# The products of probabilities and values: one block of 512 queries in the middle of a unit, or two of 256 behind every second score tile

## What is computed

```python
keys = jnp.einsum('bthk,hik->bthi', xd, tokeys) * scale
queries = jnp.einsum('bthk,hik->bthi', xd, toqueries) * scale
values = jnp.einsum('bthk,hik->bthi', xd, tovalues)
dot = jnp.einsum('bqhs,bkhs->bhqk', queries, keys)
attn = jax.nn.softmax(dot, axis=-1)
out = jnp.einsum('bhqk,bkhs->bqhs', attn, values).reshape(b, t, e)
```

## Time and profile before

| what | value |
|---|---|
| median of 3 runs | 4097.41 us |
| the runs | 4089.57 to 4101.62 us |
| the profiled execution, its time | 4100.87 us |
| its span | 4099.1 us |
| mean granted clock over the span | 0.972 |

### The profile page before, as it was taken

The page is one execution under the profiler, slowest core; times in us unless marked ns, Lnnn a source line. Parts: engine busy times, 40 slices in busy tenths (PEclk is TensorE's granted clock), DMA queues, the critical chain, the costliest instruction groups (busy, mean ns, idle before and its releaser), DMA issues. The chain is left out here.

```text
span 4099.1 us, 68353 instructions
## 1 busy us (share of the span) xinstructions
PE 3909.5 (95%) x23166; PEld 1958.1 (48%) x23166; DVE 3234.2 (79%) x3515; ACT 2628.8 (64%) x4939; POOL 455.0 (11%) x402
## 2 busy tenths in 40 slices
PE   8799899999999999999999999999998778999998
PEld 6587233333333333333333333333333656888887
DVE  6566799999898999989999989999971837765665
ACT  3454687878778787877878787788874432223333
POOL 0133100000000000000000000000001217001323
PEclk9899999999999999999999999999995888999999
DMA  4800321121021121113112112200012003004332
GB/s 146 226 21 16 107 30 19 12 24 28 9 30 27 9 25 21 21 12 34 21 9 28 26 10 23 31 9 6 9 29 54 26 0 107 1 1 133 77 84 37
DMA packets 301695, 157.53 MB, mean 38 GB/s; under 512 B 218397, under 2 KB 273507, under 8 KB 298800
## 3 DMA queue, kind: packets, MB, share of 16 engines
q1 hardware_dynamic: 289072, 142.49, 18.5%
q0 software_dynamic: 12288, 10.70, 1.6%
HBM read 86.46 MB, written 64.18 MB: 37 GB/s over the span
## 5 line engine op out<-in xcount | busy, mean ns | idle before, releaser
L1207 ACT ACTIVATE probs<-attention_scores_t_sums 128x512 f32<-128x512 f32 x4096 | 2126.2, 603 | 572.2 <-PE attention_scores_t_sums L1134 565.5
L1241 DVE TENSOR_REDUCE max_parts<-attention_scores_q_sums 128x1 f32<-128x1024 f32 x1008 | 1188.6, 1219 | 135.1 <-PE attention_scores_q_sums L1128 134.3
L1241 DVE TENSOR_REDUCE attention_max_parts<-attention_scores_q_sums 128x1 f32<-128x1024 f32 x992 | 1168.9, 1220 | 121.9 <-PE attention_scores_q_sums L1128 121.9
L1134 PE MATMUL attention_scores_t_sums<-q_operand,k_operand 50*128 50x512 f32 x2048 | 821.7, 469 | 14.9 <-ACTq L1221 14.0
L1134 PE MATMUL attention_scores_t_sums<-attention_q_operand,attention_k_operand 50*128 50x512 f32 x2048 | 827.3, 477 | 6.9 <-ACT probs L1207 6.9
L1128 PE MATMUL attention_scores_q_sums<-attention_k_operand,attention_q_operand 48*128 48x512 f32 x2048 | 666.5, 440 | 6.5 <-DVE max_parts L1241 2.6
L1128 PE MATMUL attention_scores_q_sums<-k_operand,q_operand 48*128 48x512 f32 x1952 | 636.7, 441 | 11.9 <-issue 5.7
L1128 PEld LDWEIGHTS attention_scores_q_sums<-attention_k_operand,attention_q_operand 48*128 48x128 f32 x2048 | 301.6, 185 | 576.8 <-DVE max_parts L1241 287.6
L1142 PE MATMUL attention_o_psum_sums<-probs,attention_v_heads 128*32 128x512 f32 x4104 | 564.7, 623 | 0.0
L1128 PEld LDWEIGHTS attention_scores_q_sums<-k_operand,q_operand 48*128 48x128 f32 x1952 | 289.1, 185 | 557.2 <-DVE max_parts L1241 273.4
L1142 PE MATMUL attention_o_psum_sums<-probs,v_heads 128*32 128x512 f32 x4096 | 545.5, 605 | 0.3 <-ACT o_parts L1203 0.3
(11 more groups left out here) (322 smaller groups left out, 4621.2 us busy)
## 6 DMA issues: line engine op xcount, KB each, us to landing
o_other_half<-o_parts SPq DMA_DIRECT2D x130, 64.0 KB, 2.0
expert_rows<-attention_empty_rows SPq DMA_DIRECT2D x16, 516.0 KB, 5.6
v_scratch<-value_chunk SPq DMA_DIRECT2D x16, 512.0 KB, 5.1
w_whole<-in_L_ffn_ew SPq DMA_DIRECT2D x8, 1024.0 KB, 7.2
experts_w_whole<-in_L_ffn_ew SPq DMA_DIRECT2D x8, 1024.0 KB, 5.7
q_operand<-q_scratch SPq DMA_DIRECT2D x24, 256.0 KB, 5.3
k_operand<-k_scratch SPq DMA_DIRECT2D x24, 256.0 KB, 6.5
attention_q_operand<-q_scratch SPq DMA_DIRECT2D x24, 256.0 KB, 4.8
```

The source lines that it names most:

```text
L1134: nc.tensor.matmul(ST[bank_n][:, :], KOP[b][64 * h:64 * h + ROWS + 2, kt * P:(kt + 1) * P], QOP[b][64 * h:64 * h + ROWS + 2, c * CH:(c + 1 ...
L1207: nc.scalar.activation(PR[:, tile, :], ST[bank_n][:, :], ACT.Exp).then_inc(st_free, 1)
L1241: nc.vector.tensor_reduce(MPART[par][:, h, u // 4, u % 4:u % 4 + 1], SA[h][:, :], AX.X, ALU.max)\
```

## The change

`pv_unit` becomes `pv_half`, which makes the products for 256 of the 512 queries (`side` 0 or 1). It is called behind each half of a unit, with the half's number as the side. Each call waits on ACT's count; the wait for the copy and for the values stays ahead of the first block of a round's first unit. The flag that clears the sums (`start`) is set in side 0 of unit 0 only, `pv_done` is counted behind side 1 only. The other engines' programs are the same.

```diff
-            def pv_unit(b, u, exps):
+            def pv_half(b, u, exps, side):
                 pe.wait_ge(st_free, NB + exps)
+                queries = slice(side * (CH // 2), (side + 1) * (CH // 2))
                 for t in range(4):
                     h, kt = 1 - t // 2, 2 * u + t % 2
-                    mm = nc.tensor.matmul(OP[32 * (2 * h + t % 2):32 * (2 * h + t % 2) + 32, :], VH[b][:, kt, h, :],
-                                          PR[:, u % 4 * 4 + t, :], start=(u == 0), stop=(u == U - 1))
-                mm.then_inc(pv_done, 1)
+                    mm = nc.tensor.matmul(OP[32 * (2 * h + t % 2):32 * (2 * h + t % 2) + 32, queries], VH[b][:, kt, h, :],
+                                          PR[:, u % 4 * 4 + t, queries], start=(u == 0 and side == 0),
+                                          stop=(u == U - 1 and side == 1))
+                if side == 1:
+                    mm.then_inc(pv_done, 1)
...
-                    if half == 0:
-                        if u == 1:
-                            pe.wait_ge(o_copied, g + 1)
-                            if r % NQ == 0:
-                                pe.wait_ge(v_in[r // NQ % 2], (i + 1) * 16)
-                        pv_unit((r - (u == 0)) // NQ % 2, (u - 1) % U, count(i, r, u - 2, 3) + 1)
+                    if half == 0 and u == 1:
+                        pe.wait_ge(o_copied, g + 1)
+                        if r % NQ == 0:
+                            pe.wait_ge(v_in[r // NQ % 2], (i + 1) * 16)
+                    pv_half((r - (u == 0)) // NQ % 2, (u - 1) % U, count(i, r, u - 2, 3) + 1, half)
...
-            pv_unit(1, U - 1, count(NP // 2 - 1, HALF - 1, U - 2, 3) + 1)
+            for side in range(2):
+                pv_half(1, U - 1, count(NP // 2 - 1, HALF - 1, U - 2, 3) + 1, side)
```

## The result

The changed kernel takes 3952.65 us in the median (3947.95 to 3957.45, 4 runs) against 4099.51 for the kernel before (4089.57 to 4102.72, 4 runs). The ratio is 0.9646, with a 95% interval of 0.9625 to 0.9666. The profiled execution took 3956.84 us, 144.0 less than the profiled one before.

A forecast was written before the change was run, and what follows sets the result against it. It took a loop of t2, exponential, t1 and products, 2.61 us a unit, to bound the kernel. 161 - 13 - 4.5 = 144 us less than 4100.87 gave 3957, the median 3.5 lower: 3954 us, range 3885 to 4015.

The forecast's parts named there:

- The loop before: Attention unit of the kernel before: t2, its exponential, t1, products; 1.18 + 0.42 + 1.00 = 2.60 us, the period.
- The half at full clock: Half an attention unit on PE: 0.65 us to the products plus a 0.57 us block, so a unit of 2.45.
- the term of 161 us: Gain in the attention at full clock: 2.61 - 2.45 = 0.16 us a unit, times 1006 units.
- The readers: DVE and ACT reading PE's banks: 0.4 and 0.15 us to spare, so PE itself becomes the bound.
- the sign that the prediction named: In the changed unit's timeline: DVE's idle spread over both reductions, about 0.08 us each.
- unchanged sums of ACT and DVE in the page: In the profile page: ACT's and DVE's busy sums stay the same over a shorter span.
- ACT's idle time in two parts a unit: In the changed unit's timeline: ACT idle about 0.2 us twice.
- the negated maxima's rows come in time: Row loads made half a round ahead stay hidden as eight units shrink from 20.9 to 19.6 us; cost nothing.
- The round's end: Accumulator copy and pushed exponentials delay two blocks, 0.25 us together, 0.21 more than now; times 63 rounds, 13 us.
- The last units: Last 18 attention units, without max scores, at half clock: 4.32 us a unit against 4.07, 4.5 us more.
- its second rival: Clock holds in the last units since PE stalls less: 34 us less, 3920 us; chance 0.12.
- The half at 1.2 GHz: Half a unit in the last units at half clock: 2.15 to 2.16 us, a unit 4.32.

The follow-up runs named there:

- short_exp: Kernel before, with ACT's exponentials over 256 of the 512 queries and the other probabilities constant: 3932.13 us, 0.9593 of the kernel before.
- sidebyside: Changed kernel with both blocks of 256 queries directly behind one another, behind t1: 4106.65 us, 1.0016 of the kernel before.
- quarters: Changed kernel with four blocks of 128 queries, one behind every tile: executions of 6214.52 and 6742.07 us.
- short_max: Changed kernel with DVE reducing 768 of the 1024 columns of each max score: 3946.06 us, 0.9627 of the kernel before.
- copy_late: Changed kernel with ACT copying the accumulator behind the exponential of t3 instead of t2: 3939.07 us, 0.9634 of the kernel before.
- tail_halves: Kernel before, with two half blocks in the last 24 units alone, which have no max scores: 4104.7 us, 0.9935 of the kernel before.

## Why the prediction was right, and where it wasn't

The forecast was 3954 us, the measured median 3952.65. The mechanism, a loop without its stall and PE as the new bound, was right. Two steps on the clock were not. Step by step:

- **The loop before** was read rightly: t2, its exponential, t1, products. short_exp shortens the exponential alone and the time falls; sidebyside keeps the loop and the time stays.
- **The half at full clock**, 0.65 + 0.57, was measured at 0.66 + 0.57. The split of the old block into a part that scales with the clock and one that doesn't gave the price of an additional block without an experiment, and quarters confirms it at a third size. A unit gained 0.155 us of the 0.16 forecast (2.615 to 2.46), so the term of 161 us stands within 5.
- **The readers**: PE is the bound, by short_max and quarters. The room at DVE's banks was real though its row shows none: the duration of a reduction in the record, 1.22, is longer than what a second one adds to a pair, 1.14 (two take 2.36). So the sign that the prediction named, DVE idle 0.08 ahead of each reduction, did not appear, nor did unchanged sums of ACT and DVE in the page. ACT's idle time in two parts a unit did, 0.15 each instead of 0.2. That the negated maxima's rows come in time held: no wait of PE in the attention names a DMA.
- **The round's end** was sized at 0.25 and is 0.30; both of its parts, the wait for the copy (0.11, forecast 0.08) and the pushed exponential (0.19, forecast 0.17), are shown by copy_late. The sum behind the first counts 0.65 + 0.57 + 0.07 as 1.33, which is 1.29; it doesn't say what the other 0.04 is. 13 us became about 16.
- **The last units were wrong.** The step read "the last 18 units at half clock ... 4.5 us more" and gave the clock's holding, its second rival, a chance of 0.12. The clock held, and these units gained 26.7 us beyond the common rate. The argument against it, that the work per unit is as thin as before, did not decide: the same work without the stall ahead of t1, in the changed kernel and in tail_halves, kept its clock. The argument for it, that PE stalls less, is the one that the profiles bear out.
- **The loop's ends were missing.** The prediction counted nothing there. PE's stall there was no longer than before (2.6 us against 3.0 at the first end), but the clock took up to 34 us to come back, and in the profiled execution this cost 27 us. The half at 1.2 GHz, which the prediction sized at 2.16 us for the last units, was measured here: from 1072 to 1101 us the blocks stand 2.16 us apart. Some 16 units of 4.32 us in the two stretches together, instead of 2.46, give 29 us. Why the clock comes back late stays open.

So the distance of 1 us to the median is luck: two errors of about 31 us (4.5 more became 26.7 less) and 27 us, both due to the clock, cancelled. Within one group the executions with the highest mean clock are 20 to 25 us below those with the lowest.

## What to carry to other kernels

Where a fixed number of buffers links two engines in a loop, write the loop out with its latencies from one unit of the timeline; moving part of the work from the link to the other side of the loop gains, splitting it in place does not. Price a split by the part of a block's time that doesn't scale with the clock, since every piece pays it. And count what the change does to the clock behind every stall and in every thinner stretch. Beside its price at 2.4 GHz, which is 11 us a round for quarters (50.7 against 39.67), a finer split can keep the engine from getting back to that clock (83.7 us a round).

## What the hardware showed that wasn't expected

- With four blocks a unit the granted clock stayed at 1.2 GHz for 4021 us although PE shows busy 200 of 200 us; before its fall it had run the same code at 2.4 GHz for over 800 us. The state depends on how it was entered, not on the code alone. With two blocks behind the loop's end it came back after 3.4 to 34.1 us, with one block, or two side by side, after 17.1 us at most. What exactly PE has to do to get the clock back stays open.
- In the last units the clock fell in the three profiles where PE stood still for 0.45 to 0.46 us of each unit of 2.6, and held in the ten where it stood still for 0.24 or not at all. No stall there was longer.
- Two blocks of 256 columns side by side cost under 0.01 us more than one of 512, eight more weight loads included: the loads are hidden, only the entry to the products and the way back are paid.
- DVE shows 7.38 us for six reductions in a row, no gap, and yet the unit gained nothing when each was made a fifth shorter.
